# A recommendation tower on one core: the order of work within a step, and the layers behind it set one step later

## The reference

```python
e = jnp.stack([tbl_0[ids[:, 0]], ..., tbl_25[ids[:, 25]]], axis=1)      # (512, 26, 64)
x = layer_norm(dense_t @ Wd.T, gd, bd)                                  # (512, 128)
y = layer_norm(einsum('bnd,ed->bne', e, Ws), gs, bs)
y = layer_norm(einsum('bne,pn->bep', y, Wsi), gsi, bsi)                 # norm over the 32
T = concatenate([x[:, None, :], swapaxes(y, 1, 2)], axis=1)             # (512, 33, 128)
Z = einsum('bnd,bmd->bnm', T, T)
z = layer_norm(Z[:, TRIL_I, TRIL_J] @ Wl.T, gl, bl) * mask              # 512 wide, 384 in use
h = concatenate([z, dense], axis=1)
h = maximum(h @ W_top1 + b_top1, 0);  h = maximum(h @ W_top2 + b_top2, 0)
y = h @ W_top3                                                          # (512, 1)
```

## Time and the page of the profile before

| what | us |
|---|---|
| median of three runs | 186.33 (184.78 to 186.76) |
| the profiled execution's own time | 185.44 |
| its span in the trace | 183.6 |
| PE, DVE, ACT, POOL busy in the span | 143.7, 127.4, 99.6, 105.7 |

### The profile page before, as it was taken

How to read it: one execution, slowest core, us unless ns; L and a number is a source line. 1 busy time by engine, 2 the same in 40 slices (tenths; PEclk the granted TensorE clock), 3 DMA queues, 4 the chain that set the end, 5 groups by cost and what they waited for, 6 DMA issues and landing times.

```text
span 183.6 us, 4383 instructions
## 1 busy us (share of the span) xinstructions
PE 143.7 (78%) x1693; PEld 96.5 (53%) x1693; DVE 127.4 (69%) x297; ACT 99.6 (54%) x233; POOL 105.7 (58%) x111
## 2 busy tenths in 40 slices
PE   0089877899984854899984989699859998869995
PEld 0084444525954433466652675467447654646583
DVE  6099659695989588486989497686957797730321
ACT  3003335582867585556858387755675885812130
POOL 0778777777778778778777777777773000040000
PEclk9999999999998799659999999999999999999999
DMA  4912716141111113111111221111113001020000
GB/s 135 290 49 31 300 22 199 29 118 46 34 27 26 25 25 89 38 29 28 27 26 24 66 65 26 29 31 22 28 40 77 0 5 32 12 34 3 0 0 0
DMA packets 6891, 9.58 MB, mean 52 GB/s; under 512 B 3923, under 2 KB 4056, under 8 KB 6743
## 3 DMA queue, kind: packets, MB, share of 16 engines
q0 software_dynamic: 3504, 3.46, 10.1%
q1 hardware_dynamic: 2845, 5.08, 8.5%
q10 hardware_dynamic: 522, 0.77, 1.7%
HBM read 8.01 MB, written 0.00 MB: 44 GB/s over the span
## 4 chain that ended last, share of the span: by engine, by line
POOL 46%; PE 24%; issue 17%; ACT 5%; DVE 4%; DMA 4%; ACTq 0%; DVEq 0%
POOL g_sb L239 46%; PE psW L323 5%; PE psW L347 3%; PE psH L361 3%; PE psB L293 2%; DMA ids_sb<-in_ids 2%; PE psU L281 2%; PE psZ L305 2%; ACT Zs L562 2%; DMA g_sb<-in_table,row_id 1%; DVE B L719 1%; PE psG L266 1%; ACT U L528 1%; PE psB L388 1%; DVE qA L697 1%
## 5 line engine op out<-in xcount | busy, mean ns | idle before, releaser
L239 POOL DMA_INDIRECT g_sb<-in_table,row_id x104 | 103.1, 991 | 31.7 <-issue 31.4
L562 ACT ACTIVATE Zs<-psZ 32x264 f32<-32x264 f32 x62 | 38.0, 613 | 1.1
L719 DVE TENSOR_TENSOR B<-psB,bias 128x512 f32<-128x512 f32 x32 | 20.6, 685 | 24.2 <-PE psB L293 24.2
L534 ACT ACTIVATE sqB<-B 128x512 f32<-128x512 f32 x32 | 19.7, 632 | 22.0 <-DVE B L719 20.5
L281 PE MATMUL psU<-wsi_x,g_sb 128*128 128x192 f32 (+4 forms) x128 | 22.0, 316 | 10.4 <-DVE g_sb L712 8.0
L281 PEld LDWEIGHTS psU<-wsi_x,g_sb 128*128 128x128 f32 x128 | 19.7, 194 | 16.3 <-DVE g_sb L712 12.6
L737 DVE TENSOR_TENSOR T<-B,rB 128x512 f32<-128x512 f32 x32 | 22.2, 693 | 1.1
L293 PE MATMUL psB<-U,ws_g 64*128 64x512 f32 x64 | 19.6, 692 | 3.7 <-ACT U L528 3.7
L726 DVE TENSOR_REDUCE ssB<-sqB 128x16 f32<-128x512 f32 x32 | 21.6, 678 | 0.1
L266 PEld LDWEIGHTS psG<-gram,sT 128*128 128x128 f32 x104 | 13.4, 198 | 13.4 <-ACT sT L515 10.8
L323 PE MATMUL psW<-wl_g,Zt 127*128 127x512 f32 x40 | 19.5, 621 | 0.4 <-ACT h1T L583 0.4
(11 more groups left out here) (128 smaller groups left out, 184.8 us busy)
## 6 DMA issues: line engine op xcount, KB each, us to landing
g_sb<-in_table,row_id POOLq DMA_INDIRECT x104, 2.5
wl_sb<-in_wl SPq DMA_DIRECT2D x1, 1280.0 KB, 5.5
w_sb<-in_w SPq DMA_DIRECT2D x2, 512.0 KB, 5.7
w_sb<-in_w SPq DMA_DIRECT2D x1, 768.0 KB, 4.3
small_sb<-in_small SPq DMA_DIRECT2D x1, 615.5 KB, 7.0
dense_sb<-in_dense ACTq DMA_DIRECT2D x1, 512.0 KB, 3.7
Zt<-Zs SPq DMA_DIRECT2D x3, 80.0 KB
Zt<-Zs SPq DMA_DIRECT2D x3, 70.0 KB
```

Of the source, the lines that this page charges most:

```text
L239: pool.indirect_dma_start(g_sb[:, k, h * DSP:(h + 1) * DSP], None, table, bass.IndirectOffsetOnAxis(row_id[:, 2 * k + h:2 * k + h + 1], 0) ...
L534: act.activation(sqB[:, h, :], B[:, h, :], ACT.Square).then_inc(B_squared, 1)
L562: act.activation(to, product, ACT.Copy).then_inc(Z_kept, 1)
L719: dve.tensor_tensor(B[:, h, :].rearrange("p (s j) -> p s j", j=PROJ), psB[h][:, :].rearrange("p (s j) -> p s j", j=PROJ), bias[:, :].rearr ...
```

## The change

In all three programs of the step the order is new. PE: `mix(t)`, `transposes(t+1)`, `norms(t+1)`, `inner(t-1)`, `project(t)`. DVE: the four parts for unit t+1 first, then the four for unit t. ACT: `rows_out(t+1)`, `keep_u(t)`, `enter_x(t)`, `keep_z(t-1, 0)`, `deviation_a(t+1)`, `keep_z(t-1, 1)` and 2, then the squares and roots, then `keep_z(t-1, 3)`.

The layers have another layout. `linear` computes with output features on partitions and samples in columns, in 20 products of 128 columns (`EARLY` = 12 of them at j = 0, the rest at j = 1), so nothing is transposed. The mean is taken out of the weights ahead (`wl_mean`, and `m_off` for the correcting row), so only a sum of squares is left: `squares_w` on ACT, and `variance` on PE, whose product with ones puts each sample's sum on all 128 partitions. The root and the reciprocal (`deviation_w`, `recip_w`) then are 128x128 each. The scaling comes behind layer 1 (`scale_h1`), and `hd`, which has the bias in it now, is added on DVE (`add_hd`). `w1_g` is scaled on ACT. The parts of a block are set so: j = 0 `linear` 12 of 20; j = 1 the other 8, `squares_w`, `keep_zT` (now on DVE, from `psW`); j = 2 `variance`, `deviation_w`, `layer1`; j = 3 `recip_w`, `scale_h1`, `add_hd`, `relu1`, `layer2`; j = 0 of the next block `relu2`, `output`, `copy_y`. `Zs` and `Zt` keep the two halves of a block apart, so that a relay's runs are five columns by 64 samples in one piece. In the tail the last block uses banks in pairs of features and its own `h1T_last`, `h2T_last`; the last unit's `inner` writes to `psU`.

```diff
+PS = BS // 2
+EARLY, ALL = 12, FLIN // P * CW
...
-            queue.dma_start(Zt[BASE[q]:BASE[q] + ROWS[q], b, :, lo:hi],
-                            Zs[FIRST[q] - 1:PROJ, b % 2, CW * q:CW * (q + 1), lo:hi]).then_inc(landed, 16)
+            queue.dma_start(Zt[BASE[q]:BASE[q] + ROWS[q], b, lo:hi, :, :],
+                            Zs[FIRST[q] - 1:PROJ, b % 2, lo:hi, CW * q:CW * (q + 1), :]).then_inc(landed, 16)
...
             def linear(b, lo, hi):
                 if lo == 0:
+                    pe.wait_ge(d_zt[b], 7 * 16)
+                    if b:
+                        pe.wait_ge(y_copied, b)
+                    else:
                         pe.wait_ge(x1_ready, 1)
                         pe.wait_ge(m_kept, 1)
+                for n in range(lo, hi):
+                    f, jj = n // CW, n % CW
+                    mm = pe.matmul(psW[:, f * BS:(f + 1) * BS], wl_g[0:KL, jj, f * P:(f + 1) * P],
+                                   Zt[0:KL, b, :, jj, :], start=(jj == 0), stop=(jj == CW - 1))
+                if hi == ALL:
                     mm.then_inc(W_done, 1)
+            def variance(b):
+                pe.wait_ge(W_squared, b + 1)
+                if b == 0:
+                    pe.wait_ge(bz_ready, 1)
+                elif b < LAST - 1:
+                    pe.wait_ge(h1_scaled, b)
                 else:
+                    pe.wait_ge(A_mul, UNITS)
+                for f in range(FLIN // P):
+                    mm = pe.matmul(psS[b][:, 0:BS], ones_sb[:, :], z_sq[:, f * BS:(f + 1) * BS], start=(f == 0),
+                                   stop=(f == FLIN // P - 1))
+                mm.then_inc(W_summed, 1)
+            def top1(b, f, to):
                 for k in range(KZ):
+                    mm = pe.matmul(to, w1_g[:, k, f * P:(f + 1) * P], zT[:, k * BS:(k + 1) * BS], start=(k == 0),
+                                   stop=(k == KZ - 1))
+                return mm
+            def layer1(b):
+                pe.wait_ge(zT_ready, b + 1)
+                if b < LAST - 1:
+                    pe.wait_ge(W_sd, b + 1)
+                else:
+                    pe.wait_ge(h1_scaled, b)
+                if b == 0:
+                    pe.wait_ge(w1_ready, 1)
+                for f in range(K1):
+                    mm = top1(b, f, psH[:, f * BS:(f + 1) * BS])
+                mm.then_inc(h1_done, 1)
...
             def last_block():
+                pe.wait_ge(d_zt[LAST], 10 * 16)
+                pe.wait_ge(d_zt_act, 2 * 16)
+                pe.wait_ge(d_zt_pool, 2 * 16)
+                pe.wait_ge(Z_kept, 4 * UNITS)
+                pe.wait_ge(sT_ready, UNITS)
+                for f in range(FLIN // P):
+                    for jj in range(CW):
+                        mm = pe.matmul(psL[f // 2][:, f % 2 * BS:(f % 2 + 1) * BS], wl_g[0:KL, jj, f * P:(f + 1) * P],
+                                       Zt[0:KL, LAST, :, jj, :], start=(jj == 0), stop=(jj == CW - 1))
+                    if f % 2:
+                        mm.then_inc(W_f[f // 2], 1)
+                def sums_of_squares(g):
+                    pe.wait_ge(sq_f[g], 1)
+                    for f in (2 * g, 2 * g + 1):
+                        mm = pe.matmul(psV[:, 0:BS], ones_sb[:, :], z_sq[:, f * BS:(f + 1) * BS], start=(f == 0),
+                                       stop=(f == FLIN // P - 1), skip_group_check=True)
+                    return mm
+                sums_of_squares(0)
+                pe.wait_ge(zT_f[0], 1)
+                pe.wait_ge(zT_f[1], 1)
                 pe.wait_ge(B_added, 2 * UNITS)
+                top1(LAST, 0, psF[0][:, 0:BS])
+                sums_of_squares(1).then_inc(W_summed, 1)
+                top1(LAST, 1, psF[0][:, BS:2 * BS]).then_inc(h1_f[0], 1)
+                top1(LAST, 2, psF[1][:, 0:BS])
+                top1(LAST, 3, psF[1][:, BS:2 * BS]).then_inc(h1_f[1], 1)
                 layer2(LAST - 1)
+                pe.wait_ge(W_sd, LAST)
                 for k in range(K1):
+                    if k % 2 == 0:
+                        pe.wait_ge(h1T_f[k // 2], 1)
                     for f in range(K2):
+                        mm = pe.matmul(psO[f][:, 0:BS], w2_sb[:, k, f * P:(f + 1) * P],
+                                       h1T_last[:, k * BS:(k + 1) * BS], start=(k == 0), stop=(k == K1 - 1))
                         if k == K1 - 1:
                             mm.then_inc(h2_f[f], 1)
+                output(LAST - 1)
...
                 mix(t)
                 if t + 1 < UNITS:
                     transposes(t + 1)
-                project(t)
+                if late and j == 0 and b:
+                    output(b - 1)
+                if late and j == 2:
+                    variance(b)
                 if t + 1 < UNITS:
                     norms(t + 1)
-                if t:
+                    if t:
+                        inner(t - 1)
+                project(t)
+                if t == UNITS - 1:
                     inner(t - 1)
...
                 if late and j == 0:
+                    linear(b, 0, EARLY)
                 if late and j == 1:
+                    linear(b, EARLY, ALL)
                 if late and j == 2:
+                    layer1(b)
                 if late and j == 3:
+                    layer2(b)
             for t in range(UNITS):
                 step(t)
             inner(UNITS - 1)
+            variance(LAST - 1)
+            layer1(LAST - 1)
             last_block()
...
+            def squares_w(b):
+                act.wait_ge(W_done, b + 1)
+                if b:
+                    act.wait_ge(W_summed, b)
+                act.activation(z_sq[:, :], psW[:, :], ACT.Square).then_inc(W_squared, 1)
             def deviation_w(b):
+                act.wait_ge(W_summed, b + 1)
                 if b:
                     act.wait_ge(W_recip, b)
+                bank = psS[b] if b < LAST else psV
+                act.activation(zsd[:, :], bank[:, 0:BS], ACT.Sqrt, bias=eps_c[:, :], scale=1.0 / FLIN).then_inc(W_sd, 1)
             def relu1(b):
+                act.wait_ge(h1_added, b + 1)
                 if b:
                     act.wait_ge(h2_done, b)
+                act.activation(h1T[:, :], h1[:, :], ACT.Relu).then_inc(h1_ready, 1)
...
                 late = 0 <= b < LAST
+                if late and j == 0 and b:
+                    relu2(b - 1)
                 if t + 1 < UNITS:
                     rows_out(t + 1)
+                keep_u(t)
+                if t == 3:
+                    act.wait_ge(m_shift, 1)
+                    act.wait_ge(wl_scaled, 1)
+                    act.activation(wl_g[0:NA, 0, :], psW[0:NA, :], ACT.Identity, bias=m_off[0:NA, :],
+                                   scale=g_i[0:NA, :]).then_inc(m_kept, 1)
+                if late and j == 3:
+                    relu1(b)
                 if late and j == 2:
                     deviation_w(b)
+                enter_x(t)
+                if 0 < t < UNITS - 1:
+                    keep_z(t - 1, 0)
+                if t + 1 < UNITS:
+                    deviation_a(t + 1)
+                if 0 < t < UNITS - 1:
+                    keep_z(t - 1, 1)
+                    keep_z(t - 1, 2)
                 squares_b(t, 0)
                 squares_b(t, 1)
+                deviation_b(t, 0)
+                if t == UNITS - 1:
                     keep_z(t - 1, 0)
+                deviation_b(t, 1)
+                if late and j == 1:
+                    squares_w(b)
+                if t == UNITS - 1:
                     keep_z(t - 1, 1)
                     keep_z(t - 1, 2)
                 if t:
                     keep_z(t - 1, 3)
                 if t == 0:
...
                 if t == 2:
+                    act.wait_ge(d_w1, 16)
+                    for k in range(KZ):
+                        last = act.activation(w1_g[:, k, :], w1_sb[:, k, :], ACT.Copy, scale=gl_c[:, k:k + 1])
+                    last.then_inc(w1_ready, 1)
+                if 4 <= t < 4 + K1:
+                    f = t - 4
+                    if f == 0:
+                        act.wait_ge(hd_ready, K1)
+                        act.wait_ge(bz_ready, 1)
+                    act.activation(hd[:, f, :], hd[:, f, :], ACT.Identity, bias=b1_z[:, f:f + 1]).then_inc(hd_biased, 1)
...
+            def recip_w(b):
                 dve.wait_ge(W_sd, b + 1)
+                if b:
+                    dve.wait_ge(h1_scaled, b)
                 dve.reciprocal(zr[:, :], zsd[:, :]).then_inc(W_recip, 1)
+            def scale_h1(b):
                 dve.wait_ge(W_recip, b + 1)
+                dve.wait_ge(h1_done, b + 1)
                 if b:
+                    dve.wait_ge(h1_ready, b)
+                dve.tensor_tensor(h1[:, :].rearrange("p (f s) -> p f s", f=K1),
+                                  psH[:, :].rearrange("p (f s) -> p f s", f=K1),
+                                  zr[:, :].rearrange("p (o s) -> p o s", o=1).broadcast_to([P, K1, BS]),
```

(33 more changed lines are left out.)

278 lines of the change are left out of this document (86 added, 192 removed).

## The result

| | before | after |
|---|---|---|
| median (20 runs each) | 186.2 us | 187.63 us (185.74 to 190.41) |
| profiled execution: own time, span | 185.44, 183.6 | 188.78, 187.0 |
| PE, DVE, ACT, POOL busy | 143.7, 127.4, 99.6, 105.7 | 146.7, 137.4, 108.3, 104.0 |

The ratio after to before is 1.0085, with an interval of 1.0051 to 1.0119: the changed kernel is slower by some 1.6 us. First the page: busy times, the clock in 40 slices, the chain's shares, and the four groups with the most to say (busy, mean ns, idle ahead and its releaser).

The account below looks back on a forecast made before the run. No engine full; the last 65 us were put down to the step loop and tail. Multiply 149.6, plus 12.5, tail 22.05 and clock 0.6 gave span 184.8; the execution's own time and the median made 187.5, range 182.5 to 191.5.

Parts of the forecast that it names:

- multiply to T0: Last unit, from unit 15's multiply to the end of its row scaling: 12.5 us, where before took 11.1.
- T0: End of the last row scaling into T, where the tail begins: forecast 162.1 us, 3.6 later than before's 158.53.
- T0 to the last linear: Tail, last keep_z 2.6 us and relays 4.7 us until linear starts: 7.3 us, before 9.3.
- Part 1 and 2 (the loop): Steps up to unit 15: new order's loop 7.6 us, no shorter; a block with layers 34.4 us.
- So the moved layers buy almost nothing there: Three steps from unit 12's to unit 15's multiply: 26.1 us with the moved layers, 26.4 before.
- Part 1: Step order: DVE scales the next unit (A) first, then this one's bias and norm work; loop 7.6 us, DVE idle 0.6.
- Part 6 (clock): PE's clock in the loop: new idles of some 2.4 us between transposes and norms, 0.6 us added once.
- Part 5 (tail): From the last row scaling to the end: 22.05 us, relays 1.0 off, linear to copy 13.15.
- the rival of the tail clock: PE idle 3.1 us before the last linear, back at half speed, losing 2.3: 189.8 us; chance 0.15.
- Cheaper pieces: Rival: recip_w at 0.3 us in the loop and other pieces cheaper, 183.5 us; chance 0.27.
- ACT's queue: Rival: new ACT passes ahead of rows_out lengthen each step by 0.4 us, 4.4 in eleven: 191.9 us; chance 0.08.
- The marks of "wrong": Unit 15's multiply before 146 or behind 152, tail under 21 us, or PE under 1.00 in the last 20 us.

Follow-up runs that it names:

- e3: Changed kernel plus two unused 512-column products on PE between transposes and norm products of steps 4, 5 and 6; 189.37 us, ratio 1.0256 to before.
- e1: Changed kernel with keep_z(t-1, 3) moved from the end of ACT's step to behind rows_out of the next step; 184.38 us, ratio 0.9934 to before.
- e4: Changed kernel without ACT's four passes over hd in steps 4 to 7, so without biases b1 and bl; 186.82 us, ratio 1.0072 to before.
- e2: Changed kernel with its new layers but the step order of the kernel before; 180.47 us, ratio 0.9784 to before.
- e7: Changed kernel, new order kept, work ahead of rows_out and norms moved behind them on ACT, PE and DVE; ratio 0.987 to before, again 0.9887.

## Why the prediction was right

The forecast was 187.5 us, within 182.5 to 191.5, and it came to 187.63; the reading, "a wait for project becomes a wait for norms through ACT's queue, and the loop is no shorter", is what the rows show. But the sum came out by errors of both signs, and by luck. Its terms, from the profiled execution:

| step | predicted | measured |
|---|---|---|
| unit 4's multiply | 55.95 | 55.99 |
| unit 12's multiply | 123.5 | 126.58 |
| a block (units 8 to 12) | 34.4 | 126.58 - 91.75 = 34.83 |
| unit 12's to unit 15's | 26.1 | 152.73 - 126.58 = 26.15 |
| unit 15's multiply | 149.6 | 152.73 |
| multiply to T0 | 12.5 | 13.5 |
| T0 to the last linear | 7.3 | 5.74 |
| linear to the end of the copy | 13.15 | 185.37 - 171.99 = 13.4 |
| tail | 22.05 | 20.75 |
| clock | 0.6 | no row of its own: in the rows above, 2 to 3 before unit 8 with ACT's queue, up to 1 behind unit 15's multiply |
| span | 184.8 | 187.0 |
| from span to the median | +2.7 | +0.6 |

- **The last row is luck.** The span came out 2.2 us above the sum, and the median hit all the same. To the span I added 1.8 for the execution's own time and 0.9 because before's profiled execution lay 0.9 below its median; after's lies 1.15 above its own. An execution at the median would have a span of some 185.9, 1.1 above the sum.
- **Part 1 and 2 (the loop).** Right by their rows: the wait moved as named, the steps of units 12 to 15 took 8.66, 9.23 and 8.26 for 8.45, 9.2 and 8.45, and recip_w cost 0.94 to 0.95 for the 0.95 taken from the slope of two small shapes. The 8.45 of the first is a four-slot loop and squares_w; variance's 0.95 is named there but isn't in it. The Trainium skill (VectorE: DVE Perf Modes, "First, the fixed hardware budget") has Reciprocal as an iterative divide. The trace agrees that it is no plain pass (0.94 against 0.29 us), and the estimate of 1.07 worked out from it was a little high.
- **"So the moved layers buy almost nothing there"** is the sentence that failed. Compared with the old steps, new layers in the new order came out level, and I put that down to the layers. The table of four shows two large parts: the layers give 4.0 us in the old order (between the two profiled executions 5.4: 4.7 in the tail and 1.7 from unit 11 to 15, less 1.0 before), and the order costs 5 to 6 with them and 8 to 9 without. Part 1, which found the new order "no shorter", should have said by how much it is longer: it had DVE idle 0.6 us in each turn, where the waits for norms came to 1.3 and the one for A's root to 0.4.
- **Part 6 (clock).** Mis-sized: 0.6 was added, and unit 12's multiply is 3.1 late, 2.7 of it between units 4 and 8, where windows of 0.74, 0.50 and 0.65 granted lie. e3 gives 2.2 us of it back by filling the idles, and e1 as much by clearing one copy out of ACT's queue. The row was there to see it (2.33 us idle, then 0.50), and Part 6 itself named the new idles of 2.4 us.
- **Part 5 (tail).** POOL's two relays, the only ones whose landing the trace has, landed 1.8 and 2.0 us after their issue, the far bound (2.5 off 4.5), where I had taken 1.0 off. POOL's two issues together took 1.09 for 2.27. Idle ahead of linear is 1.21, not 3.1, so the rival of the tail clock had no ground: 1.00 granted through the tail. The Trainium skill (TensorE: Matmul & The Clock Gate, "What's actually happening") has the throttled state as the default, which activity releases. The trace agrees in the loop, where 0.50 was granted behind two of the idles and 0.97 to 1.00 again under work; the tail has no such fall.
- **Rivals.** "Cheaper pieces" did not come: recip_w cost its upper bound, and keep_z took 619 ns against 613. "ACT's queue" was right in kind, for e1 gains 2.8 by one copy less ahead of rows_out; most of its price stood already in the forecast's loop, and hd's pass, named for it, was worth nothing to be seen (e4).
- **The marks of "wrong"** fired twice: a multiply behind 152, a tail under 21. Each was right about its term, and their errors cancelled: +4.15 at T0, -1.3 in the tail, -0.6 for the clock term counted apart, +2.25 in the span.

Shown: the order costs more than the layers give, and some 3 us of it are one copy ahead of rows_out; in steps that no gather bounds, all that stands ahead of rows_out and norms is worth 5. Open: the 3 us that the new order loses up to unit 3, what DVE's wait for the root of A costs, how much of the loss is the clock's, and why e3 is slower as a whole. The best version is e2, the new layers with the old order, at 0.9784; e7's edits on it without the late copy_y were not tried.
